# Softmax row sums taken from TensorE products with ones, in a one-core decoder layer

## The reference

```
scores = einsum('bhgqd,bhkd->bhgqk', q, k) * scale
scores = where(causal, scores, -inf)
attn = softmax(scores, axis=-1)
out = einsum('bhgqk,bhkd->bhgqd', attn, v)
```

## Time and profile before

| | |
|---|---|
| median of 3 runs | 1601.74 us (1595.86 to 1602.22) |
| the profiled execution | 1596.27 us, its span 1594.5 us |
| busy in the span | PE 1382.6 us (87%), DVE 1108.9 us (70%), ACT 689.2 us (43%), POOL 112.0 us (7%) |
| mean granted TensorE clock | 0.888 of full speed |
| attention of batch 0 | about 78 to 250 us of the span |
| attention of batches 1, 2, 3 | about 536 to 617, 906 to 990, 1278 to 1362 us |

### The profile page before, as it was taken

The page is one execution under the profiler, slowest core; times in us unless marked ns, Lnnn a source line. Parts: engine busy times, 40 slices in busy tenths (PEclk is TensorE's granted clock), DMA queues, the critical chain, the costliest instruction groups (busy, mean ns, idle before and its releaser), DMA issues.

```text
span 1594.5 us, 16051 instructions
## 1 busy us (share of the span) xinstructions
PE 1382.6 (87%) x5768; PEld 675.0 (42%) x5768; DVE 1108.9 (70%) x1247; ACT 689.2 (43%) x1501; POOL 112.0 (7%) x116
## 2 busy tenths in 40 slices
PE   6756667999988799899989699899989698799999
PEld 2334334444443355434444255444434255454443
DVE  4899996557989775737999866637998967621120
ACT  6155653344543484343552376361562277321110
POOL 0000001000200000000210000100210000100000
PEclk8955558999999699999999778999999869789999
DMA  4166662114667631113766722002566751101112
GB/s 191 40 152 157 141 142 50 42 50 112 172 145 172 171 68 27 40 35 81 180 147 159 196 67 54 27 32 80 141 150 152 169 139 28 27 19 61 50 35 84
DMA packets 53277, 158.80 MB, mean 100 GB/s; under 512 B 5072, under 2 KB 10704, under 8 KB 44752
## 3 DMA queue, kind: packets, MB, share of 16 engines
q0 software_dynamic: 9216, 67.11, 20.4%
q1 hardware_dynamic: 25664, 54.23, 10.1%
q10 hardware_dynamic: 18320, 36.45, 8.6%
HBM read 86.20 MB, written 4.46 MB: 57 GB/s over the span
## 4 chain that ended last, share of the span: by engine, by line
issue 30%; PE 29%; DVE 26%; DMA 7%; ACT 5%; POOL 2%; ACTq 0%; DVEq 0%; POOLq 0%
DVE state L1082 10%; DMA y_sb<-state 7%; PE ps_a L890 5%; PE ps_a L970 4%; DVE state L1077 4%; PE ps_w L869 3%; DVE state L1087 3%; PE ps_a L816 3%; PE ps_a L902 2%; PE ps_b L830 2%; ACT r L622 2%; POOL rstd L474 2%; DVE neg_max L1117 2%; PE ps_b L910 2%; PE ps_w L778 2%
## 5 line engine op out<-in xcount | busy, mean ns | idle before, releaser
L890 PE MATMUL ps_a<-xt,w_sb 128*128 128x512 f32 x704 | 316.1, 603 | 0.0
L1082 DVE TENSOR_TENSOR_SCAN state<-decay,state 128x2048 f32<-128x2048 f32 x64 | 282.8, 4419 | 7.5 <-ACT decay L580 3.4
L1253 DVE TENSOR_TENSOR r<-r,ps_a 128x512 f32<-128x512 f32 x132 | 88.6, 683 | 206.4 <-ACT r L674 206.4
L816 PE MATMUL ps_a<-r 32*128 32x512 f32 (+3 forms) x512 | 140.6, 634 | 84.0 <-ACT r L622 57.5
L890 PEld LDWEIGHTS ps_a<-xt,w_sb 128*128 128x128 f32 x704 | 135.6, 194 | 171.1 <-issue 171.1
L674 ACT ACTIVATE r<-ps_a 128x512 f32<-128x512 f32 x132 | 78.4, 597 | 297.8 <-PE ps_a L902 158.7
L580 ACT ACTIVATE decay<-dt_sb,decay_rate 128x511 f32<-128x511 f32 x256 | 163.0, 712 | 63.2 <-DVE state L1087 31.2
L622 ACT ACTIVATE r<-ps_a,neg_max 128x128 f32<-128x128 f32 (+3 forms) x256 | 133.8, 534 | 118.7 <-DVE neg_max L1117 118.3
L902 PE MATMUL ps_a<-r,wb_sb 128*128 128x512 f32 x352 | 166.7, 596 | 11.1 <-DVE r L1253 8.9
L970 PE MATMUL ps_a<-wd_sb,r 128*128 128x512 f32 x352 | 161.8, 611 | 0.8 <-DMA wd_sb<-in_w_down 0.8
L1077 DVE TENSOR_TENSOR state<-du_sb,bc_sb 128x2048 f32<-128x2048 f32 x64 | 146.3, 2287 | 5.2 <-DMA y_sb<-state 5.0
(11 more groups left out here) (123 smaller groups left out, 1448.4 us busy)
## 6 DMA issues: line engine op xcount, KB each, us to landing
y_sb<-state POOLq DMA_DIRECT2D x64, 1024.0 KB, 9.7
bc_sb<-bc_rows ACTq DMA_DIRECT2D x64, 512.0 KB, 5.1
w_sb<-in_w_tiles SPq DMA_DIRECT2D x44, 512.0 KB, 4.0
wd_sb<-in_w_down SPq DMA_DIRECT2D x44, 256.0 KB, 3.6
wb_sb<-in_w_adapt SPq DMA_DIRECT2D x44, 128.0 KB, 2.1
xa<-in_x SPq DMA_DIRECT2D x4, 1024.0 KB, 5.2
out_x<-xb SPq DMA_DIRECT2D x16, 256.0 KB, 7.0
xn_att<-in_ctx_t SPq DMA_DIRECT2D x4, 512.0 KB, 6.1
```

Source lines behind the costliest of these rows:

```text
L816: nc.tensor.matmul(score_place(s, k), q_t[rows, m, i * P:(i + 1) * P], k_t[rows, 0:width], start=True, stop=False, tile_position=(rows.sta ...
L890: mm = nc.tensor.matmul(ps_a[:, 2 * (f % 2) + half, :], w_sb[:, slot, at + k * P:at + (k + 1) * P], xt[:, k, :], start=(k == 0), stop=Fals ...
L1082: nc.vector.tensor_tensor_scan(flat, decay[:, n % 2, :, :].rearrange("p j l -> p (j l)"), flat, 0.0, ALU.mult, ALU.add).then_inc(scan_chai ...
```

## The change

The exponents are no longer summed by ScalarE. In a group, TensorE multiplies the transposed exponents first with a 128 x 32 block of ones, into the second 128 columns of the bank, and then with v, into the first 128. So each row sum comes out in all 32 rows of its head, where its inverse is needed. VectorE takes the reciprocal of this 128 x 128 block from PSUM and multiplies by it. The inversions of two sums a step, the spreading products, ScalarE's copy and the waits on them go; a memset of the ones is added at the start.

```diff
-        row_sum = sb("row_sum", [P, 2, 2])
-        row_inv = sb("row_inv", [P, 4, HPT])
+        ones = sb("ones", [P, HD])
...
                 def exponents(s):
                     i = (s // 2) % NT
                     act.wait_ge(neg_max_ready, b * STEPS + s + 1)
-                    if s >= 2:
-
-                        act.wait_ge(inv_chain, b * STEPS + s - 1)
...
                                              score_place(s, k), ACT.Exp,
-                                             bias=neg_max[:, s % 2, k:k + 1],
-                                             accum_out=row_sum[:, s % 2, k:k + 1]).then_inc(exp_done, 1)
+                                             bias=neg_max[:, s % 2, k:k + 1]).then_inc(exp_done, 1)
...
-                def move_output(g):
-                    m, i = g // NT, g % NT
-                    bank = filled(act, ("pv", g), b)
-
-                    nc.scalar.activation(attn_t[:, m, i * P:(i + 1) * P], ps_w[:, bank, P:2 * P], ACT.Copy)\
-                        .then_inc(inv_moved, 1)
...
                     pe.wait_ge(pt_ready, b * 2 * STEPS + 4 * g + 4)
-                    pe.wait_ge(inv_chain, b * STEPS + 2 * g + 2)
-                    for j in range(HPT):
-                        nc.tensor.matmul(ps_w[j * HD:(j + 1) * HD, bank, P:2 * P],
-                                         row_inv[:, g % 4, j:j + 1].to_broadcast([P, HD]), ident,
-                                         start=True, stop=True, tile_position=(0, j * HD))
-                    for kt in range(i + 1):
-                        for j in range(HPT):
-                            mm = nc.tensor.matmul(ps_w[j * HD:(j + 1) * HD, bank, 0:P],
-                                                  v_sb[:, kt, j // 2 * HD:(j // 2 + 1) * HD],
-                                                  probs_t[4 * (g % 2) + j][:, kt * P:(kt + 1) * P],
-                                                  start=(kt == 0), stop=(kt == i), tile_position=(0, j * HD))
+                    for at, weights in ((P, None), (0, v_sb)):
+                        for kt in range(i + 1):
+                            for j in range(HPT):
+                                w = ones[:] if weights is None else weights[:, kt, j // 2 * HD:(j // 2 + 1) * HD]
+                                mm = nc.tensor.matmul(ps_w[j * HD:(j + 1) * HD, bank, at:at + P], w,
+                                                      probs_t[4 * (g % 2) + j][:, kt * P:(kt + 1) * P],
+                                                      start=(kt == 0), stop=(kt == i), tile_position=(0, j * HD))
...
-                def invert_sums(s):
-                    dve.wait_ge(exp_done, b * 2 * STEPS + 2 * s + 2)
-                    nc.vector.reciprocal(row_inv[:, (s // 2) % 4, 2 * (s % 2):2 * (s % 2) + 2], row_sum[:, s % 2, :])\
-                        .then_inc(inv_chain, 1)
-
                 def divide(g):
                     m, i = g // NT, g % NT
-                    bank = use(("pv", g), b)[0]
-                    dve.wait_ge(inv_moved, b * MT * NT + g + 1)
+                    bank = filled(dve, ("pv", g), b)
                     place = attn_t[:, m, i * P:(i + 1) * P]
+                    nc.vector.reciprocal(place, ps_w[:, bank, P:2 * P]).then_inc(inv_chain, 1)
+                    dve.wait_ge(inv_chain, b * MT * NT + g + 1)
                     tt(place, ps_w[:, bank, 0:P], place, ALU.mult).then_inc(work_free[bank], 1)
...
+            nc.vector.memset(ones[:], 1.0).then_inc(consts_ready, 1)
...
```

More of the change, by code:

```diff
@@ L311, in decoder_layer @@
         pv_done = sem("pv_done")
-        inv_moved = sem("inv_moved")
         x1_ready = sem("x1_ready")
@@ L649, in attention @@
                         exponents(s)
-                    for g in value_groups(s):
-                        move_output(g)
                     if s < STEPS:
@@ L984, in _ @@
             project_dt(0, range(JT))
-            pe.wait_ge(consts_ready, 4)
+            pe.wait_ge(consts_ready, 5)
             pe.wait_ge(loaded["att"], 64)
@@ L1144, in attention @@
                         maxima(s)
-                    if 1 <= s <= STEPS:
-                        invert_sums(s - 1)
                     if s < STEPS:
@@ L1269, in _ @@
             dve.wait_ge(loaded["vec"], 16)
+            nc.vector.memset(ones[:], 1.0).then_inc(consts_ready, 1)
             ts(q_bias[:], vec[:, V_BQ:V_BQ + MT], SCALE, None, ALU.mult)
             ts(conv_half[:], vec[:, V_CW:V_CW + 20], 0.5, None, ALU.mult).then_inc(conv_halved, 1)
-            dve.wait_ge(consts_ready, 1)
+            dve.wait_ge(consts_ready, 2)
             ts(decay_rate[:], decay_rate[:], -1.0, None, ALU.mult).then_inc(consts_ready, 1)
@@ L1275, in _ @@
             convolve(0, range(JT))
-            dve.wait_ge(consts_ready, 4)
+            dve.wait_ge(consts_ready, 5)
             dve.wait_ge(loaded["x"], 16)
```

## The result

The changed kernel takes 1618.72 us (median of 4 runs, 1612.65 to 1622.20) against 1601.53 (1595.86 to 1602.22): ratio 1.0116, 95% interval 1.0096 to 1.0136. It is slower by 15 to 22 us. That is inside the range of 1614 to 1660, about half of the forecast step of 36 us, and under the 1626 to 1652 that the prediction gave its main case alone. The profiled execution grew from 1594.5 to 1616.1 us of span, so by 21.6.

The account below looks back on a forecast made before the run. VectorE was taken to bound batch 0 and TensorE batches 1 to 3, VectorE briefly at scan steps. 1596.27 + 15 (batch 0) + 24 (later batches) = 1635 us, put at 1638 as median; range 1614 to 1660.

Parts of the forecast that it names:

- main case: Whole kernel: dear reciprocal and both regimes as told, 1626 to 1652 us, chance 0.66.
- two regimes: Attention: VectorE sets batch 0 one for one; TensorE paces batches 1 to 3, VectorE momentarily where a scan stands.
- dear reciprocal: VectorE's reciprocal of the spread sums was to cost about 1.32 us each, against 0.29 if cheap.
- clock rows: TensorE's clock in batches 1 to 3: the forecast counts as wrong if its row falls under 0.80.
- cheap reciprocal: Rival: the reciprocal costs 0.29 us like a product, +20 us in all, 1619 us; chance 0.12.
- Both parts of the sum: Batch 0's attention +15 us; that of batches 1 to 3 about 8 us each, +24 us.
- The reciprocal of 128 x 128: VectorE, each group: 141 ns fixed plus 9.25 ns a number, 1.32 us; bounds 0.29 and 1.42.
- The tail's 1.5: Batch 0, last three groups behind the scan pieces: TensorE's products with ones add 1.1 to 2.3 us, taken as 1.5.
- ScalarE's part: Losing copy and accumulator saves 0.09 us for each of two exponents, 0.2 us a step, only at scan steps.
- TensorE's products: Batches 1 to 3: extra products with ones, 0.21 us per 8 records, 5.0 us a stage plus 1.3 at half clock.
- a rival for the worse only: Batches 1 to 3: longer TensorE waits behind scans keep its clock at 1.2 GHz, +20 us, 1658; chance 0.09.
- The reciprocal in batches 1 to 3: Hidden in VectorE's free time except at scan steps 11, 15, 27: 1.0 us each, 1.5 us more a stage.

Follow-up runs that it names:

- e6: Changed kernel with VectorE's reciprocal made a second time behind the first in each group: 1659.5 us, ratio 1.0390 to the kernel before.
- e10: Changed kernel with the inverse made by ScalarE as exp(-ln(sum)) in place of VectorE's reciprocal: 1682.2 us, ratio 1.0515 to the kernel before.
- e9: Changed kernel with the products with ones made twice, the second time into a free quarter of the bank: 1631.2 us, ratio 1.0196.
- e3: Kernel before without the accumulator of ScalarE's exponents (sums a constant 1, output not normalised): 1591.2 us, ratio 0.9946.
- e2: Changed kernel with one set of products with ones a group instead of one per key tile (output not normalised): 1615.3 us, ratio 1.0114.
- e5: Kernel before with i extra, unread sets of products with ones in each group: 1612.7 us, ratio 1.0093.
- e7: Kernel before without the exponents' accumulator and with the copy of the inverses made by VectorE in all batches: 1598.9 us, ratio 1.0012.
- e8: Kernel before with only the copy of the inverses moved to VectorE, in batches 1 to 3: 1608.8 us, ratio 1.0044.
- e13: Changed kernel with the change undone in batch 0, batches 1 to 3 as changed: 1612.2 us, ratio 1.0083 to the kernel before.

## Why the prediction held, and what in it was off

**What held, and what was luck.** The direction, the two regimes and the dear reciprocal held, and the clock rows stayed over 0.80. The number is inside the range by the range's width. 1618.7 lies under the main case's own 1626, and on the 1619 of the cheap reciprocal, a rival that is false (0.29 us; 0.95 was measured). Both parts of the sum, batch 0's and that of the later batches, were put too high. Of the prediction's own signs, the stages 1 to 3 were to grow by 6 to 10 us each and grew by 3; batch 0 was to grow by 15 and not by less than 10, and grew by 10.5 in the profile and by 1 to 10 by the medians.

**Two regimes, VectorE's work one for one in batch 0.** Right: e6 (12.5 of 12.9 us), e10 (-2.4 with the reciprocal gone) and e9 (31 more sets, +0.9) each show it.

**The reciprocal of 128 x 128.** Mis-sized: 0.95 us instead of 1.32. I drew a line through two very short sizes; from two to 128 numbers it is (950 - 158)/126 = 6.3 ns a number, not 9.25. With 0.95 + 0.04 - 0.16 = 0.83 a group, 13 x 0.83 - 2.4 = 8.4 us, and 8.8 were measured in the steps. The tail's 1.5 was 1.8. So the stage grew by 10.5 us and not 15. The Trainium skill's repeat count of 8 (VectorE: DVE Perf Modes, First, the fixed hardware budget) had given an estimate of 1.21 us; 0.95 us was measured, and that decides. Its sign was the useful part: the cheap rival at 0.29 us was wrong.

**ScalarE's part.** Two steps failed, both in batches 1 to 3, and this is the first: I gave 0.2 us at three steps of a stage and said ScalarE "isn't what either regime waits for". e3 shows 2.9 us a stage (1.9 in the batch where the clock gave nothing), 0.54% of the whole. The mistake was to read 0.09 us as a saving where TensorE's waits are listed. The exponents are in a ring with scores and maxima that has 64 of them a stage, 5.8 us in all, and up to half of it came through.

**TensorE's products.** The second step that failed, and the larger: "Nothing hides this in steps without scans." The 0.21 us per 8 records were right and the 6.3 us a stage were not; in the changed kernel e2 and e9 give 0.03 to 0.11 us a set. TensorE had been early at the scores behind those three pieces, and the added work ate 0.66 us of each wait. The clock had been put down as a rival for the worse only, and may have given back part of the rest. In the kernel before the price was nearer the forecast (e5, +10 to +19.5 us in all), and why the two kernels differ is open.

**The reciprocal in batches 1 to 3.** From e7 to e2 (its two small inversions and a copy against the reciprocal) the steps grew by 2.7 us; I had 1.5 for the three scan steps, beyond the products. The waits behind the pieces of steps 11, 15 and 27 grew by 0.6 us each (batch 2: 0.48, 1.71 and 2.60 to 1.08, 2.32 and 3.20), so 1.8 of the 2.7 are where the forecast had put 1.0 each. So a stage adds up as 78.9 - 2.9 (accumulator) + 0.8 (copy to VectorE) + 2.7 (reciprocal) + 0.6 (products) = 80.1, a chain of single profiles, and with the tails and shifts 3.2, 3.2 and 2.8 us.

**The sum.** By the profile 15 became 10.5 and 24 became 9.2. The direction rested on the reciprocal and on VectorE being full in batch 0, and both held. No version beat the kernel before: e3 is faster because it leaves the sums out.

## What to carry to other kernels

A reading that every iteration of a ring makes can be worth up to its time times the iterations, even where the engine that makes it is part idle (here 1.9 to 3.5 of 5.8 us); test it by leaving it out. Before added work is priced in full, look at whether its engine is early at a later wait. Before an operation is moved to the engine that is full in one stage, price it at its real width in that stage: a helper result that is cheap as a column costs 6.3 ns for every number when it is spread. And a wait that disappears (14 us here) is not a gain unless something behind it was waiting.

## What the runs showed of the hardware

- Reciprocal on VectorE, float32 from PSUM: 0.95 us for 128 numbers a row, where a copy took 0.285 and a product 0.29. Against the 0.158 us for two numbers that is 6.3 ns for each further number.
- Logarithm and exponential in turn made the compiler load a table ahead of each, 1.28 us each time.
- A stall of TensorE of 1.73 us was followed by some 20 us at 1.2 GHz in two batches of e8 and by 3.4 us in the third; one of 1.65 us by 7 us in one batch of e13 and by none in the others.
- An identical program part can differ by 8 us between batches of one execution (e8: steps of 86.3, 86.2 and 78.5 us, with 49, 49 and 31 us of them at 1.2 GHz).
